# Clearing the scatter rows ahead of the FFN weights, and low parts, routing and stores reordered in a two-layer cross-attention, FFN and mixture-of-experts kernel

## Chip, cores and metric

One core of one Trainium2 chip runs the whole program in one launch. The metric is the device time in microseconds of that core. Engines: TensorE (PE), VectorE (DVE), ScalarE (ACT), GpSimd (POOL) and SyncE (SP, which only issues transfers and waits). Sixteen DMA engines serve the queues of SP, ScalarE and GpSimd.

## What is computed

Two layers over x of 2 x 256 tokens by 512, with a context of 2 x 512 by 512:

```python
x = x + xattn0(layernorm(x), ctx)   # quantised matmul
x = x + ffn0(layernorm(x))          # 4-bit block-quantised weights, 1376 wide, activations requantised
x = x + xattn1(layernorm(x), ctx)   # 32 heads, 8 KV heads, head 128, rms-normed q and k, softmax
x = x + moe1(layernorm(x))          # below

def moe1(x):                                   # 512 tokens
    scores = softmax(x @ router_w + router_b) + router_bias        # 16 experts in 4 groups
    # keep the 2 best groups, take the 2 best experts of them: idx, vals
    for e in range(16):                        # inner width 128
        h = silu(x @ w1[e] + b1[e]) * (x @ w2[e] + b2[e])
        y += gate[:, e, None] * (h @ w3[e] + b3[e])
    z = silu(x @ sw1 + sb1) * (x @ sw2 + sb2) @ sw3 + sb3          # shared expert, inner width 256
    return y + z
```

The FFN's weights are in reference form `w_gate`, `w_up` (1376, 512) and `w_down` (512, 1376).

## The kernel before

All float32 products are split: an operand is a 16-bit high part and a 16-bit low part, and `product` makes three matmuls (high x high, high x low, low x high). A high part is a copy by ScalarE, a low part is the difference, by VectorE or GpSimd. Every engine runs its own program in order, and semaphores join them. SBUF is one tensor, `arena`, cut by hand with `carve(kib, ...)`; tiles whose lives don't overlap share bytes.

**Start and FFN (0 to about 300 us).** SP's queue (from L379): inputs, the first of four 1 MB chunks of the k and v weights (`kw_load`), then the first `RAW` = 7 raw FFN weight tiles (`ring(n)`, 256 KB each), then `kw_load(1)`, which waits until the low part of the chunk before is made, `ring(7)`, `kw_load(2)`. Then the loop over `NCH` = 33 weight tiles (11 up, 11 gate, 11 down): `turn_w(n)` transposes the finished high and low part of tile n by DMA from `wt` (three slots, `DQ`) into `wfx`, `ring(n + 8)` loads a raw tile, and for n < 23 a *clear* follows: `sp.dma_start(blocks[n], blank)` writes 256 KB of zeros, DRAM to DRAM, into 128 rows of `xs_d`, the buffer into which tokens are scattered later (`blank` is a 32-row padding block of zeros in the weights, broadcast four times; `blocks[n]` is seen as 4 x 32 x 512). On the compute engines a tile goes: block maxima (VectorE), divide (GpSimd), round (ScalarE twice), `scale_back` (GpSimd), `weight_high` (ScalarE), low (VectorE, or GpSimd), `turn_w`, then TensorE's `tile`: 4 products, 12 matmuls of 128 x 512. `v_unit`s and `k_unit`s (12 matmuls each too) stand between tiles; seven of the v units stand between the first and the last of the 22 up and gate tiles. `parameters(k)` (spread on TensorE, L1199 and L1201) needs the extrema of all tiles of a matrix.

**Attention (about 300 to 657 us).** 32 steps (8 KV heads x 4 token tiles) in a loop; each has scores, softmax over VectorE, ScalarE and GpSimd, high and low parts of the probabilities (`p_high`, `p_low`), four DMA transposes (`turn_p`) and the products. Between steps (7, 1) and (7, 2) VectorE prepares the router weights and the experts' biases (L1917 to L1928).

**Experts and routing (about 640 to 700 us).** `EX` = 18 expert weight sets of 768 KB (two shared, sixteen routed) come into `ER` = 4 raw slots `me_raw` (`load_experts(n)` waits for the low part of n - 4), and get a high part (`expert_high`, ScalarE) and a low part: of those in `POOL_LOW` = (0, 1, 4, 7, 13, 15, 17) by GpSimd (which scales first), of the others by VectorE (`expert_lows`). After the last attention step VectorE makes the statistics, `expert_norm` writes `xn`, which shares bytes with the probabilities and so waits for their last transposes; TensorE transposes it, `router`, `logits`, `scores`, `choose` (the two best experts and their one-hot rows `chosen`), `earlier` (how many tokens stand before one with the same expert), `place` (the row of each token, `places`). TensorE works on the shared experts' `shared_hidden` between them. GpSimd scatters each token's row to two places (`spread_rows`, 8 indirect transfers) once all clears are in (`filled`).

**Blocks (about 700 to 781 us).** 23 blocks of 128 rows: `x_load(i)` transposes a block from `xs_d` (four slots; the first waits for the whole scatter), TensorE `tile_hidden(i)`, ScalarE `tile_sigmoid`, VectorE `tile_gate`, ScalarE `tile_hidden_high`, VectorE `tile_low`, TensorE `tile_out`, ScalarE `tile_result` into one of three `yb`, SP `y_store`. Beside blocks 0 to 9 the remaining experts' parts are made: ScalarE takes expert i + 9 after block i. Then GpSimd gathers two result rows a token, VectorE adds them, and SP stores `out`.

Of the kernel before, what the change touches and what calls it, by code (L numbers as in the profile page):

```python
# [15 lines left out]
P = 128  # L16
# [40 lines left out]
ER = 4  # L57
SC = 8
POOL_LOW = (0, 1, 4, 7, 13, 15, 17)
# [76 lines left out]
def block_kernel(nc, x, ctx, ctx_t, quant_par, ident_in, ffn_w, kv_w, mask, norm_w, wq, wo,  # L136
                 router_w, router_b, moe_w, moe_b, moe_b3, tri_in, out):
    es = ExitStack()
    with es:
# [81 lines left out]
        gt = carve(202, (1, TOK))  # L221
# [7 lines left out]
        xs = [carve(k, (2, D), F16) for k in (36, 38, 190, 192)]  # L229
        xg = [carve(194 + 2 * i, (2 * KD, P), F16) for i in range(XB)]  # L230
# [8 lines left out]
        pick_f, iota_1 = carve(102, (NE,)), carve(102.25, (NE,))  # L239
# [139 lines left out]
        def _(sp):  # L379
# [33 lines left out]
            kw_load(0)  # L413
            for n in range(RAW):
                ring(n)
            kw_load(1)
            ring(RAW)
            kw_load(2)

# [101 lines left out]
            def y_store(i):  # L521
                sp.wait_ge(t_ev, i + 1)
                sp.dma_start(y_d[i * P:(i + 1) * P], yb[i % YB]).then_inc(y_st[i % YB], 16)

# [12 lines left out]
            for i in range(TILES - XB - 3, TILES):  # L537
                y_store(i)
# [7 lines left out]
        def _(g):  # L546
# [200 lines left out]
            def expert_scale(n):  # L747
                g.wait_ge(in_me[n % ER], 16 * (n // ER + 1))
                g.tensor_scalar(me_raw[:, n % ER], me_raw[:, n % ER], SW, 1.0, ALU.mult, ALU.mult).then_inc(m_sc, 1)

            def expert_low(n):
                g.wait_ge(m_hi, high_count(n))
                g.tensor_tensor(me[n][:, 1], me_raw[:, n % ER], me[n][:, 0], ALU.subtract).then_inc(m_lo[0], 1)

# [28 lines left out]
            def xs_low(t):  # L783
                g.wait_ge(xs_hi, t + 1)
                g.tensor_tensor(xs[t][:, 1], xn[:, t], xs[t][:, 0], ALU.subtract).then_inc(xs_lo, 1)
# [8 lines left out]

            expert_scale(4)
            expert_low(4)
            rstd(6, 0, NT - 1)
            expert_scale(7)
            for t in range(NT - 1):
                xs_low(t)  # L800
            rstd(7, NT - 1, NT)
            expert_low(7)
# [5 lines left out]
            for n in (13, 15, 17):  # L808
                expert_scale(n)
                expert_low(n)  # L810
# [9 lines left out]
        def _(a):  # L820
# [265 lines left out]
            expert_high(4)  # L1086
            expert_high(5)

            def xs_high(t):
                a.wait_ge(h_nm, NT + t + 1)  # L1090
                copy(xs[t][:, 0], xn[:, t]).then_inc(xs_hi, 1)
# [11 lines left out]
            expert_high(6)  # L1103
# [7 lines left out]
            expert_high(7)  # L1111
# [38 lines left out]

            for i in range(TILES):
# [4 lines left out]
                if i + 9 < EX:  # L1156
                    expert_high(i + 9)
            for i in range(TILES - 3, TILES):
                tile_result(i)


        @block.tensor
        def _(pe):
# [239 lines left out]
            def expert_transposes(t):  # L1403
                pe.wait_ge(h_nm, NT + t + 1)
                for k in range(KD):
                    mm = pe.transpose(bank(t)[:, k * P:(k + 1) * P], xn[:, t, k * P:(k + 1) * P], ident[:, :])
# [47 lines left out]
            expert_transposes(NT - 1)  # L1454
            pe.wait_ge(h_lo, 2 * NT)
            router(NT - 1, NT)
            for i in range(2):
                shared_hidden(0, i, TOK - P, TOK)
            pe.wait_ge(m_lo[0], 2)
            shared_hidden(1, 0, 0, TOK)  # L1460
            pe.wait_ge(const_v, 4)
            pe.wait_ge(r_oh, 1)
            for t in range(NT - 1):
                earlier(t)
            pe.wait_ge(r_oh, 2)
# [4 lines left out]
            shared_hidden(1, 1, 0, TOK)  # L1470
# [63 lines left out]
        def _(v):  # L1534
# [336 lines left out]
            def attention_step(j, s):  # L1871
# [8 lines left out]
                for h in range(R):  # L1880
                    v.wait_ge(a_e, 4 * u + h + 1)
# [9 lines left out]
                final = isinstance(j, int) and u == HK * NT - 1  # L1891
                for h in range(R):
                    if final and h == 2:
                        o_low(u - 1)
                    p_low(u, h)
                if not final and (not isinstance(j, int) or u >= 1):
# [10 lines left out]
            for s in range(5):  # L1907
                attention_step(0, s)
# [5 lines left out]
            attention_step(HK - 1, 1)  # L1914

            v.wait_ge(in_mp, 16 * 5)
            own.mark(v.memset(flat(bias_raw), 0.0))  # L1917
            own.link(v.tensor_reduce(iota, tri, AX.X, ALU.add))
            own.mark(ts(later_row, iota, -float(P), ALU.mult, float((NE - 1) * P), ALU.add))
            own.link(ts(flat(mbs[:, :, :]), flat(mb[:, :, :]), SXW, ALU.mult))  # L1920
            own.link(v.tensor_copy(bias_raw[:, :, 0:NE], mb[:, :, NS:EX]))
            v.tensor_copy(bias_raw[:, :, 32:32 + NE], mb[:, :, NS:EX]).then_inc(r_ws, 1)
            own.mark(ts(b3[0:NE + 1, 0], b3[0:NE + 1, 0], SXW, ALU.mult))
            own.link(ts(flat(rw_raw), flat(rw_raw), SW, ALU.mult))
            v.tensor_copy(flat(rw[0]), flat(rw_raw)).then_inc(r_ws, 1)
            v.wait_ge(r_ws, 2)
            tt(flat(rw[1]), flat(rw_raw), flat(rw[0]), ALU.subtract).then_inc(r_ws, 1)

            attention_step(HK - 1, 2)
# [18 lines left out]
            def expert_norm(k, lo, hi):  # L1948
                v.wait_ge(rstd_ready, k + 1)
                for t in range(lo, hi):  # L1950
                    ts(xn[:, t], xres[:, t], mv[:, t, 0:1], ALU.subtract, rs[:, t:t + 1], ALU.mult).then_inc(h_nm, 1)
# [24 lines left out]
            def choose(lo, hi):  # L1976
                n = hi - lo
# [5 lines left out]
                own.wait(own.n)  # L1983
                own.link(v.tensor_copy(at[:, lo:hi], best_at[:, lo:hi, 0:2]))
# [30 lines left out]
            own.mark(ts(pick, pick_f, SW, ALU.mult))  # L2015
            for t in range(3):
# [5 lines left out]
            expert_norm(7, 3, 4)  # L2022
# [4 lines left out]
            own.link(ts(iota_1, iota, 1.0, ALU.add))  # L2027
            own.link(tt(pick_f, pick_f, iota_1, ALU.mult))
            own.link(v.tensor_reduce(part, pick_f, AX.X, ALU.add))
# [152 lines left out]
```

## Time and profile before

| | |
|---|---|
| runs, median (lowest to highest) | 811.12 us (808.1 to 814.69) |
| the profiled execution | 807.26 us, span 805.4 us |
| busy: TensorE, VectorE, GpSimd, ScalarE | 647.5 (80%), 626.9 (78%), 531.1 (66%), 494.0 us (61%) |
| share of 16 DMA engines, SP's queue | 63.3% of the span |

The page gives the span in 40 slices of about 20 us, one digit of busy tenths each; TensorE's are at 9 from slice 17 to slice 31. "PEclk" is TensorE's granted clock. A wait "[4.01 <-DVE ...]" is the engine's idle time before an instruction and what ended it. Transfers on a queue have no duration as such: the SP timeline shows the time in which SP issued them, and "us to landing" is from the issue to the semaphore.

### The profile page before, as it was taken

To read this page: it belongs to the slowest core of one execution; us is meant where nothing else is said; L and a number is where in the kernel's file an instruction comes from. 1 tells how busy PE (TensorE), PEld (TensorE's weight loads), DVE (VectorE), ACT (ScalarE), POOL (GpSimd) and SP (SyncE) were. 2 spreads that over 40 slices of the span, in tenths; PEclk is the share of its full clock that TensorE was granted. 3 is DMA by queue.
4 is the path that set the end of the run, shared out by engine and by line. 5 is a ranking of instruction groups with operands and counts; after the bars stand their busy time and mean duration, and the time that the engine had idled before them with its cause. 6 is when DMAs were issued, how large, how long until landed. Compare 5 with 4: busy or idle time off the path is not lost.

```text
span 805.4 us, 12660 instructions
## 1 busy us (share of the span) xinstructions
PE 647.5 (80%) x3432; PEld 316.6 (39%) x3432; DVE 626.9 (78%) x1331; ACT 494.0 (61%) x986; POOL 531.1 (66%) x505
## 2 busy tenths in 40 slices
PE   0595898846395996999999999999999868676870
PEld 0242343312132442444444444444444335254650
DVE  6896687788899678788888888888888876476622
ACT  4564665659757437777777777777777763145430
POOL 1897586887666557788788888888888744405004
PEclk9899999988688898999999999999999988888995
DMA  8326999992434315877766667666645670499944
GB/s 342 103 81 83 188 188 202 178 166 53 92 59 93 123 58 146 179 169 180 181 142 143 149 156 156 156 143 143 143 92 104 109 244 1 138 289 271 218 145 157
DMA packets 231272, 120.12 MB, mean 149 GB/s; under 512 B 213933, under 2 KB 214189, under 8 KB 228286
## 3 DMA queue, kind: packets, MB, share of 16 engines
q1 hardware_dynamic: 229950, 115.42, 63.3%
q0 software_dynamic: 1280, 4.20, 1.6%
q8 instruction: 20, 0.33, 0.2%
q14 instruction: 22, 0.18, 0.1%
HBM read 57.97 MB, written 15.20 MB: 91 GB/s over the span
## 4 chain that ended last, share of the span: by engine, by line
PE 49%; DVE 20%; DMA 9%; issue 8%; POOL 7%; ACT 4%; SPq 2%; POOLq 0%; DVEq 0%; ACTq 0%
PE ps L1166 16%; PE ps L1168 15%; PE ps L1167 15%; DVE arena L1541 5%; DVE arena L1544 4%; DMA arena<-arena 3%; ACT arena L822 3%; DVE arena L1538 2%; DMA y_d<-arena 2%; POOL arena L594 1%; PE ps L1334 1%; DMA arena<-in_moe_w 1%; POOL arena L586 1%; DVE ss L1691 1%; DMA arena<-in_ffn_w 1%
## 5 line engine op out<-in xcount | busy, mean ns | idle before, releaser
L1166 PE MATMUL ps<-arena 128*128 128x512 f16 (+2 forms) x1011 | 360.6, 361 | 74.2 <-DMA arena<-arena 26.0
L1167 PE MATMUL ps<-arena 128*128 128x512 f16 (+2 forms) x1011 | 359.6, 360 | 0.0
L1168 PE MATMUL ps<-arena 128*128 128x512 f16 (+2 forms) x1011 | 358.6, 359 | 0.0
L822 ACT ACTIVATE arena<-arena 128x512 f16<-128x512 f32 (+8 forms) x404 | 249.2, 649 | 88.1 <-POOL arena L767 29.6
L1166 PEld LDWEIGHTS ps<-arena 128*128 128x128 f16 (+1 forms) x1011 | 102.1, 101 | 191.8 <-issue 51.0
L1538 DVE TENSOR_TENSOR arena<-arena 128x512 f16<-128x512 f32 (+3 forms) x163 | 126.6, 807 | 22.5 <-ACT arena L822 22.2
L1168 PEld LDWEIGHTS ps<-arena 128*128 128x128 f16 (+1 forms) x1011 | 102.5, 101 | 102.2 <-issue 9.8
L1167 PEld LDWEIGHTS ps<-arena 128*128 128x128 f16 (+1 forms) x1011 | 102.3, 101 | 90.4 <-issue 7.2
L767 POOL TENSOR_SCALAR arena<-arena,rden 128x512 f32<-128x512 f32 x128 | 114.5, 894 | 16.1 <-DVE rden L1884 6.8
L1044 ACT ACTIVATE arena<-arena,mneg 128x512 f32<-128x512 f32 x124 | 88.6, 715 | 35.1 <-DVE mneg L1864 35.1
L822 ACT ACTIVATE arena<-ps 128x512 f16<-128x512 f32 (+2 forms) x105 | 58.7, 587 | 52.6 <-PE ps L1168 29.5
L1864 DVE CUSTOM_DVE_ANT_0 arena<-ps,arena 128x512 f32<-128x512 f32 x128 | 82.9, 685 | 3.4 <-issue 0.3
L715 POOL TENSOR_TENSOR arena<-arena 128x512 f32 (+1 forms) x64 | 73.3, 1165 | 8.1 <-ACT arena L822 8.1
L1544 DVE SCALAR_TENSOR_TENSOR arena<-arena 128x128 f16<-128x128 f32 (+7 forms) x62 | 54.0, 887 | 26.7 <-DMA arena<-y_d,places 15.6
L730 POOL TENSOR_TENSOR rk<-ss,nh 128x4 f32<-128x4 f32 x32 | 32.6, 1018 | 50.1 <-DVE ss L1541 50.0
L710 POOL TENSOR_SCALAR arena<-arena 128x512 f32<-128x512 f32 x64 | 60.3, 955 | 2.4
L1544 DVE SCALAR_TENSOR_TENSOR arena<-ps,arena 128x512 f16<-128x512 f32 (+3 forms) x80 | 52.0, 655 | 7.0 <-ACT arena L822 4.7
L594 POOL TENSOR_TENSOR arena<-arena,dsc 128x512 f32<-128x512 f32 x33 | 38.8, 1176 | 6.6 <-ACT arena L822 6.6
L1538 DVE TENSOR_TENSOR arena<-ps,arena 128x128 f32<-128x128 f32 (+2 forms) x51 | 16.1, 319 | 34.4 <-ACT arena L1137 32.7
L586 POOL TENSOR_TENSOR arena<-arena,dsi 128x512 f32<-128x512 f32 x33 | 37.0, 1121 | 5.8 <-DVE dsi L1582 5.8
L815 POOL DMA_INDIRECT arena<-y_d,places x8 | 8.6, 1072 | 41.8 <-DMA y_d<-arena 39.7
L1541 DVE TENSOR_SCALAR arena<-arena,aqp 128x512 int32<-128x512 f32 x48 | 34.4, 721 | 0.3
(156 smaller groups left out, 722.5 us busy)
## 6 DMA issues: line engine op xcount, KB each, us to landing
arena<-in_moe_w SPq DMA_DIRECT2D x18, 768.0 KB, 5.5
arena<-in_ffn_w SPq DMA_DIRECT2D x33, 256.0 KB, 6.0
arena<-in_wq SPq DMA_DIRECT2D x8, 1024.0 KB, 5.1
arena<-in_wo SPq DMA_DIRECT2D x8, 1024.0 KB, 5.1
xs_d<-in_ffn_w SPq DMA_DIRECT2D x23, 256.0 KB
y_d<-arena SPq DMA_DIRECT2D x23, 256.0 KB, 3.0
arena<-in_kv_w SPq DMA_DIRECT2D x4, 1024.0 KB, 7.6
arena<-arena SPq DMA_TRANSPOSE x177, 3.3
```

The source lines that it names most:

```text
L710: g.tensor_scalar(src, src, SW, 1.0, ALU.mult, ALU.mult).then_inc(aw_sc, 1)
L715: g.tensor_tensor(lo, src, hi, ALU.subtract).then_inc(aw_lo, 1)
L767: g.tensor_scalar(sc[:, h], sc[:, h], rden[:, h:h + 1], SP, ALU.mult, ALU.mult)\
L822: return a.activation(out_, in_, ACT.Copy, scale=scale, bias=bias)
L1044: a.activation(sc[:, h], sc[:, h], ACT.Exp, bias=mneg[:, h:h + 1], scale=-1.0, accum_out=den[:, h:h + 1]).then_inc(a_e, 1)
L1166: pe.matmul(out_, lhs[0], rhs[0], start=first, stop=False)
L1167: pe.matmul(out_, lhs[0], rhs[1], start=False, stop=False)
L1168: return pe.matmul(out_, lhs[1], rhs[0], start=False, stop=last)
L1538: return v.tensor_tensor(out_, x_, y_, op)
L1541: return v.tensor_scalar(out_, x_, s1, s2, o1, o2)
L1544: return v.scalar_tensor_tensor(out_, x_, s_, y_, o1, o2)
L1864: v.tensor_tensor_reduce(sc[:, h], bank(h), mk[:, t % 2], -1.0 / SXW, 3.0e38, ALU.add, ALU.min, mneg[:, h:h + 1]).then_inc(a_sm, 1)
```

## The change

- **Clears**: out of the weight loop; 7 behind the seventh raw load, 8 behind `kw_load(1)`, 8 behind `kw_load(2)`, all ahead of `turn_w(0)`.
- **Low parts**: `POOL_LOW` is (0, 1) only; experts 2 to 7 are done by VectorE behind the routing and the shared hidden parts, 8 to 17 one per block. High parts on ScalarE follow.
- **Five raw slots**: `ER` = 5. `load_experts(5)` stands ahead of the last `turn_p`, then 4 (whose slot shares bytes with attention operands) and 6 to 12, all ahead of SP's wait for the scatter.
- **Routing**: the norm writes `xe_n` (108 KB, free by then) in three pieces of 2, 1 and 1 tiles; the one-hot rows (`mark`) are split from `choose`; TensorE leaves the last token tile's columns of all shared products for after the counts; small operands are made elsewhere.
- **Bias and router operands**: spread over attention steps (0, 1) to (0, 4), (7, 1) and (7, 2), each ahead of the last reciprocal of the step.
- **Last attention step**: the four `p_high` and `p_low` are no longer interrupted by an expert's high part or `o_high`, `o_low`.
- **Stores**: `y_store(i)` is issued from ScalarE's queue, behind block i + 3's work.

```diff
-ER = 4
+ER = 5
-POOL_LOW = (0, 1, 4, 7, 13, 15, 17)
+POOL_LOW = (0, 1)
...
             for n in range(RAW):
                 ring(n)
+            clear(0, 7)
             kw_load(1)
+            clear(7, 15)
             ring(RAW)
             kw_load(2)
+            clear(15, TILES)
...
-                if n < TILES:
-                    sp.dma_start(blocks[n], blank).then_inc(filled, 16)
...
             turn_p(HK - 1, 2)
+            load_experts(5)
+            turn_p(HK - 1, 3)
+            sp.wait_ge(a_y, HK * NT - NT)
             load_experts(4)
-            turn_p(HK - 1, 3)
-            for n in range(5, 9):
+            for n in range(6, 13):
                 load_experts(n)
...
-            for n in range(9, 12):
-                load_experts(n)
             for i in range(TILES - XB):
                 x_load(i + XB)
-                if i + 12 < EX:
-                    load_experts(i + 12)
-                if i >= 3:
-                    y_store(i - 3)
+                if i + 13 < EX:
+                    load_experts(i + 13)
...
              for h in range(R):
-                if h == 2:
-                    expert_high(2)
-                    o_high(last - 1)
                 p_high(last, h)
+            o_high(last - 1)
+            expert_high(2)
             expert_high(3)
...
             shared_sigmoid(0)
-            expert_high(8)
+            shared_sigmoid(1)
+            expert_high(5)
+            expert_high(6)
             shared_high(0)
-            shared_sigmoid(1)
+            expert_high(7)
             a.wait_ge(g_t, 1)
             copy(gt[0:NE + 1, 0], bank(0)[0:NE + 1, :]).then_inc(g_c, 1)
             shared_high(1)
+            for n in range(8, 12):
+                expert_high(n)
...
                 tile_hidden_high(i)
-                if i + 9 < EX:
-                    expert_high(i + 9)
+                if i + 12 < EX:
+                    expert_high(i + 12)
+                if i >= 3:
+                    y_store(i - 3)
...
+            pe.wait_ge(m_lo[0], 2)
+            shared_hidden(1, 0, 0, TOK - P)
             pe.wait_ge(h_lo, 2 * NT)
             router(NT - 1, NT)
-            for i in range(2):
-                shared_hidden(0, i, TOK - P, TOK)
-            pe.wait_ge(m_lo[0], 2)
-            shared_hidden(1, 0, 0, TOK)
...
             earlier(NT - 1).then_inc(r_rank, 1)
-            shared_hidden(1, 1, 0, TOK)
+            for n in range(NS):
+                for i in range(2):
+                    shared_hidden(n, i, TOK - P, TOK)
...
-            expert_lows(2)
             stats(0, 2)
-            expert_lows(3)
+            variance(0, 2)
             add_out(HK - 1, 2)
             stats(2, 3)
-            variance(0, 3)
-            for h in range(R):
-                v.wait_ge(turned[h], 16 * HK * NT)
-            expert_norm(6, 0, 3)
-            o_low(HK * NT - 1)
+            variance(2, 3)
+            expert_norm(6, 0, 2)
+            expert_norm(7, 2, 3)
...
+            v.wait_ge(xs_lo, NT)
             shared_hidden(0)
             gates()
+            expert_lows(2)
             shared_low(0)
             shared_hidden(1)
+            expert_lows(3)
             shared_low(1)
-            expert_lows(5)
-            expert_lows(6)
+            for n in range(4, 8):
+                expert_lows(n)
...
-                if i in beside:
-                    expert_lows(beside[i])
                 tile_low(i)
+                if i + 8 < EX:
+                    expert_lows(i + 8)
```

## Rows read from the trace of the kernel before

**Rows 1.** Windows view: us, busy time (instructions) per engine, PEclk, DMA share, GB/s

```profile
30.00:35.00 5.00, 1.27 (x6) 0.39 (x4) 4.00 (x8) 2.56 (x4) 5.00 (x5) 0.96 0.00 0
150.00:160.00 10.00, 7.32 (x35) 2.96 (x32) 8.12 (x13) 6.83 (x12) 10.00 (x10) 1.00 0.94 166
```

**Rows 2.** SP's timeline, 0 to 160 us: start, us, queue, line, operation, count

```profile
4.03 21.33 SPq L395 DMA_DIRECT2D arena<-in_ffn_w  x7
36.89 0.33 SPq L404 DMA_DIRECT2D arena<-in_kv_w  x1
...
56.02 0.33 SPq L404 DMA_DIRECT2D arena<-in_kv_w  x1
67.99 1.35 SPq L410 DMA_TRANSPOSE arena<-arena  x1
...
70.00 0.85 SPq L431 DMA_DIRECT2D xs_d<-in_ffn_w  x1
```

**Rows 3.** DMA view, 70 to 100 us, in 40 slices of 0.75 us

```profile
DMA  9689231349992295992269924299922699222992
GB/s 170 180 187 119 79 71 66 99 104 332 281 153 98 99 235 99 296 200 109 98 156 318 327 106 108 93 300 309 195 106 101 153 321 313 109 98 93 293 273 98
```

**Rows 4.** Windows view, half a microsecond inside one clear

```profile
99.50:100.00 0.50, 0.50 (x4) 0.20 (x2) 0.50 (x2) 0.50 (x2) 0.38 (x1) 1.00 0.25 98
```

**Rows 5.** Source view of the weight transposes (L410): 135 to 171, 171 to 215 us

```profile
DMA to landing us min/median/max: 3.9/5.6/7.1
...
DMA to landing us min/median/max: 3.0/3.1/5.0
```

**Rows 6.** TensorE's timeline: tile 0, tile 4, the next unit, the gate's spread

```profile
71.29 0.38 PE L1166 MATMUL ps<-arena 128*128 128x512 f16 x1 [1.57 <-DMA arena<-arena]
...
90.86 0.39 PE L1166 MATMUL ps<-arena 128*128 128x512 f16 x1 [1.35 <-DMA arena<-arena]
93.46 0.38 PE L1166 MATMUL ps<-arena 128*128 128x512 f16 x1
...
176.92 0.37 PE L1199 MATMUL ps<-ident,ext 128*2 128x128 f32 x1 [5.09 <-DVE ext L1654]
```

**Rows 7.** Waits, 71 to 171 us: us in total, times, longest

```profile
PE ps L1166 <- DMA arena<-arena: 20.5, 15, 3.9
```

**Rows 8.** VectorE's timeline, 626 to 686 us

```profile
627.74 0.27 DVE L1917 MEMSET arena<- 128x256 f32 x1
...
629.71 0.23 DVE L1538 TENSOR_TENSOR arena<-arena 128x64 f16<-128x64 f32 x1
...
652.93 3.86 DVE L1544 SCALAR_TENSOR_TENSOR arena<-arena 128x1536 f16<-128x1536 f32 x1
...
670.02 3.31 DVE L1541 TENSOR_SCALAR arena<-arena,mv,rs 128x512 f32<-128x512 f32 x1 [0.32 <-POOL rs L556]
...
682.22 0.17 DVE L1541 TENSOR_SCALAR arena<-ps 128x16 int32<-128x16 f32 x1 [3.09 <-PE ps L1467]
...
684.72 0.17 DVE L1544 SCALAR_TENSOR_TENSOR places<-arena 128x8 int32<-128x8 f32 x1
```

**Rows 9.** The chain that ended last, 700 to 760 us: start, us, what

```profile
715.66 1.68 DVE arena L1544
...
726.79 3.99 DVE arena L1544
```

**Rows 10.** Page (loads to landing); timelines of SP and ScalarE, 699 to 780 us

```profile
arena<-in_moe_w SPq DMA_DIRECT2D x18, 768.0 KB, 5.5
...
699.62 5.55 SPq L519 DMA_TRANSPOSE arena<-xs_d  x4
...
705.75 0.28 ACT L1137 ACTIVATE arena<-ps 128x128 f32<-128x128 f32 x1 [15.35 <-PE ps L1504]
...
710.83 1.48 ACT L822 ACTIVATE arena<-arena 128x1536 f16<-128x1536 f32 x1 [3.81 <-DMA arena<-in_moe_w]
...
779.39 0.28 ACT L1137 ACTIVATE arena<-ps 128x128 f32<-128x128 f32 x1 [1.23 <-PE ps L1504]
```

More of the change, by code:

```diff
@@ L228, in block_kernel @@
         gsc = carve(165.953125, (NT, 2))
-        xs = [carve(k, (2, D), F16) for k in (36, 38, 190, 192)]
-        xg = [carve(194 + 2 * i, (2 * KD, P), F16) for i in range(XB)]
+        xs = [carve(k, (2, D), F16) for k in (36, 38, 150, 152)]
+        xg = [carve(196 + 2 * i, (2 * KD, P), F16) for i in range(XB)]
+        xe_n = carve(108, (NT, D))
         yb = [carve(k, (D,)) for k in (100, 102, 162)]
@@ L413, in _, with clear @@
             kw_load(0)
+            def clear(lo, hi):
+                for n in range(lo, hi):
+                    sp.dma_start(blocks[n], blank).then_inc(filled, 16)
             for n in range(RAW):
                 ring(n)
+            clear(0, 7)
             kw_load(1)
+            clear(7, 15)
             ring(RAW)
             kw_load(2)
+            clear(15, TILES)
             def turn_k(u):
@@ L1405, in expert_transposes @@
                 for k in range(KD):
-                    mm = pe.transpose(bank(t)[:, k * P:(k + 1) * P], xn[:, t, k * P:(k + 1) * P], ident[:, :])
+                    mm = pe.transpose(bank(t)[:, k * P:(k + 1) * P], xe_n[:, t, k * P:(k + 1) * P], ident[:, :])
                 mm.then_inc(h_ps, 1)
@@ L1869, in p_low, with attention_step @@
                 tt(ph[:, h, 1], sc[:, h], ph[:, h, 0], ALU.subtract).then_inc(a_pl, 1)
-            def attention_step(j, s):
+            def attention_step(j, s, beside=None):
                 u, t = 4 * j + s, s % 4
@@ L1880, in attention_step @@
                 for h in range(R):
+                    if beside and h == R - 1:
+                        beside()
                     v.wait_ge(a_e, 4 * u + h + 1)
@@ L1890, in attention_step @@
                     tile_low(NT - 1)
-                final = isinstance(j, int) and u == HK * NT - 1
                 for h in range(R):
-                    if final and h == 2:
-                        o_low(u - 1)
                     p_low(u, h)
-                if not final and (not isinstance(j, int) or u >= 1):
+                if not isinstance(j, int) or u >= 1:
                     o_low(u - 1)
@@ L1906, in _, with bias_rows, bias_columns, out_biases @@
             tile_norm(3)
-            for s in range(5):
-                attention_step(0, s)
+            def bias_rows():
+                v.wait_ge(in_mp, 16 * 5)
+                own.mark(v.memset(flat(bias_raw), 0.0))
+                ts(flat(mbs[:, :, :]), flat(mb[:, :, :]), SXW, ALU.mult)
+            def bias_columns():
+                own.mark(v.tensor_copy(bias_raw[:, :, 0:NE], mb[:, :, NS:EX]))
+                v.tensor_copy(bias_raw[:, :, 32:32 + NE], mb[:, :, NS:EX]).then_inc(r_ws, 1)
+            def out_biases():
+                own.mark(ts(b3[0:NE + 1, 0], b3[0:NE + 1, 0], SXW, ALU.mult))
+            def router_scaled():
+                own.mark(ts(flat(rw_raw), flat(rw_raw), SW, ALU.mult))
+                own.mark(v.tensor_reduce(iota, tri, AX.X, ALU.add))
+            def router_high():
+                v.tensor_copy(flat(rw[0]), flat(rw_raw)).then_inc(r_ws, 1)
+                own.mark(ts(later_row, iota, -float(P), ALU.mult, float((NE - 1) * P), ALU.add))
+            def router_low():
+                v.wait_ge(r_ws, 2)
+                tt(flat(rw[1]), flat(rw_raw), flat(rw[0]), ALU.subtract).then_inc(r_ws, 1)
+            attention_step(0, 0)
+            attention_step(0, 1, bias_rows)
+            attention_step(0, 2, bias_columns)
+            attention_step(0, 3, out_biases)
+            attention_step(0, 4, router_scaled)
             def four_steps(j):
@@ L1913, in _ @@
             own.loop(1, HK - 1, 4, four_steps)
[L1914 to L1929, printed above, removed]
+            attention_step(HK - 1, 1, router_high)
+            attention_step(HK - 1, 2, router_low)
             attention_step(HK - 1, 3)
@@ L2026, in _ @@
             logits(3, 4, 1)
-            own.link(ts(iota_1, iota, 1.0, ALU.add))
-            own.link(tt(pick_f, pick_f, iota_1, ALU.mult))
-            own.link(v.tensor_reduce(part, pick_f, AX.X, ALU.add))
-            own.link(ts(part, part, -1.0, ALU.add))
+            mark(0, 3)
             scores(3, 4, 1)
             choose(3, 4)
+            mark(3, 4)
+            own.mark(v.memset(gts[:, :, 0:NS], 1.0))
+            own.mark(ts(gsc, best[:, :, 0:2], 1.0 / SXW, ALU.mult))
             place()
@@ L2050, in gates @@
                 tops = best[:, :, 0:2]
-                own.mark(v.memset(gts[:, :, 0:NS], 1.0))
-                own.mark(ts(gsc, tops, 1.0 / SXW, ALU.mult))
                 own.link(tt(where, chosen, tops.unsqueeze(3).broadcast_to([P, NT, 2, NE]), ALU.mult))
                 tt(gts[:, :, NS:EX], where[:, :, 0], where[:, :, 1], ALU.add).then_inc(gates_ready, 1)
+            v.wait_ge(xs_lo, NT)
             shared_hidden(0)
             gates()
+            expert_lows(2)
             shared_low(0)
             shared_hidden(1)
+            expert_lows(3)
             shared_low(1)
-            expert_lows(5)
-            expert_lows(6)
+            own.link(ts(iota_1, iota, 1.0, ALU.add))
+            own.link(tt(pick_f, pick_f, iota_1, ALU.mult))
+            own.link(v.tensor_reduce(part, pick_f, AX.X, ALU.add))
+            own.link(ts(part, part, -1.0, ALU.add))
+            for n in range(4, 8):
+                expert_lows(n)
             def extra_tiles():
```

54 lines of the change are left out of this document (19 added, 35 removed).

## The prediction

> **What bounds the kernel now.** I read the page first: TensorE is busy 80% of the span, and its digits of the forty slices stand at 9 from about 320 to 625 us alone. In that attention stretch it has no room to give, and the change takes nothing from it. The edits lie in the loads at the start, the FFN stretch, the last attention step, the routing, and the 23 expert blocks.
>
> *Start.* The windows view shows the DMA engines doing nothing at 30 to 35 us [rows 1], and the SP queue's timeline shows why: after the seven first raw loads (issue ends at 25.4 us) SP waits for results, and sends only one wk/wv chunk at 36.9, another at 56.0 and, at 68.0, the first weight transpose [rows 2]. That is the room into which the change puts 23 clears.
>
> *FFN.* From 70 to 100 us the DMA view alternates between full bars and bars of 2 tenths at about 98 GB/s, one such dip per FFN tile [rows 3]; a half-microsecond window inside one dip has share 0.25 and 98 GB/s [rows 4]. Those dips are the clears: a quarter of the 16 engines works, which is what the source's outermost dimension of 4 (the zero block repeated four times) gives. So a clear of 262 KB takes 262/98 = 2.67 us, and what stands behind it on SP's queue waits: a weight transpose lands in 5.6 us while clears run between them, in 3.1 us once they are over [rows 5]. TensorE starts its first tile at 71.29 and another at 90.86, four later: 4.9 us each, where the twelve matmuls of a tile need 93.46 - 90.86 = 2.60 us [rows 6]. Over 71 to 171 us its matmuls waited 20.5 us for these transposes [rows 7]. The stretch ends at VectorE's extrema, at 176.92.
>
> *Tail.* VectorE's timeline and the chain show two costs around the routing: the low parts of experts 2 and 3 stand ahead of the norm, and an instruction of VectorE takes 3.86 or 3.31 us where GpSimd multiplies or subtracts beside it [rows 8]; a 1536-wide low part takes 1.68 us alone and 3.99 beside GpSimd [rows 9].
>
> **The change, part by part.**
>
> *Clears moved ahead.* Seven go behind the seventh raw load, eight behind the chunk of 36.9 us, eight behind that of 56.0. Nothing is removed: 23 x 2.67 = 61.4 us of a quarter of the engines, and every load and transpose here uses all 16, so each waits at the clears before it. In order on those four engines, with the first clear's data 2 us after its issue (an estimate from the 3.1 us in which an undisturbed transpose is issued, run and reported): 7 clears from 27.4 to 46.1; the chunk, 1,049 KB at four times the dip's rate (4 x 98 = 392 GB/s), 2.7 us, to 48.8; 8 clears to 70.2; raw load 7 and the third chunk, 0.7 + 2.7, to 73.6; the last 8 clears, 21.4, to 95.0. Only then comes the first weight transpose, issued at 68 as before: with 2.0 us more to run and report (3.1 from issue to landing when undisturbed [rows 5], 1 of them before the data), TensorE's first tile starts at 97.0 instead of 71.3, **+25.7**. That the second chunk comes 7 us late delays GpSimd's scaling and the v units behind it, but all of it is over well before 95.0 and hides there. Bounds: nothing, if successive clears run beside each other on other engines (a rival below); +30 if some clears run slower.
>
> What is given back: with no clears between tiles, the queue holds about 0.7 (raw load) + 1.3 (transpose, my estimate from the same 3.1) per tile, under TensorE's 2.6. The most that can come back is TensorE's idle time. From tile 0 to the end of the gate tiles it has 22 tiles and 7 v units, 29 x 2.60 = 75.4 us of work; in before this took from 71.29 to 176.92 - 5.09 = 171.8, so 25.1 us were idle [rows 6], 20.5 of them on transposes [rows 7]. I take 15.0 back, not 20.5: GpSimd is busy for 10.00 of 10.00 us at 150 to 160 [rows 1], so the later transposes are also late because their weights are, and after 20 us without work the ring of three weight slots has to fill again. Ends: 8 (only the first ten tiles gain) and 23.8 (TensorE almost without a gap). **Net of the stretch: 25.7 - 15.0 = +10.7**, between +1.9 and +18. What comes after (gate, product, down projection) is a chain of results and starts later by as much.
>
> By the Trainium skill, "DMA: Bandwidth & Descriptors", section "Rules for kernel authors", a transfer whose outermost dimension is a repeat of c copies stays on at most c engines, and the section "Why a DMA increments its semaphore by 16 and not by 1" adds that from SP's queue these are always the lowest-numbered ones. The first half is what the bars show; the second no row here can show, as no two clears of before run back to back. With the second the sum stays +10.7; without it the clears would need 23 x 0.67 = 15.4 us, and the first rival below would hold.
>
> *Bias and router operands.* Ten small VectorE instructions between attention steps (from 627.74 to 629.94, 2.2 us [rows 8]) go into steps 0 to 4 and two late steps. There they stand where VectorE waits for an exponential anyway. TensorE did not stop at once for them; I take **-1.2** at the end, and +0.7 in the first steps, where nobody is at 100% yet. Ends: 0 and -2.2; 0 and +2.2.
>
> *Last step and routing.* The norm no longer waits behind the two low parts (1.68 + 3.86), its own copy no longer takes 3.31 instead of about 0.7 (GpSimd's low part beside it is gone), and TensorE's counts no longer stand behind shared-expert products, for which VectorE waited 3.09 [rows 8, 9]. Together 1.7 + 3.9 + 2.6 + 3.1 = 11.3: the places, ready at 684.9 now [rows 8], come 11 us sooner relative to the attention, and the scattered rows with them.
>
> *What is late next.* SP must issue the loads of experts 6 to 12 before it waits for the scatter, and load n waits for the low part of expert n - 5. The low parts of 2 to 7 now all stand on VectorE behind the places, and the order has a link through the loads: low 2, then load 7 (5.5 us to land [rows 10]), then ScalarE's high part 7 (1.48 [rows 10]), then the second shared hidden, and only then lows 4 to 7. From places at 673.9 (in before's times): shared hidden, gates and low 2 to 678.4; load 7 to 684.4; high 7 and two copies to 687.1; shared low and four small ones to 688.6; four lows at 1.68 to 695.3. Load 12 is issued then and x transpose 0 after it, at 696 where it was 699.62 [rows 10], and it runs behind 10 to 12, three loads of 786 KB. So block 0's sigmoid comes at 705, where it came at 705.75 [rows 10]: **-0.7** of the 11 arrives. Ends: -8 if the loads are quick, +3.
>
> *Blocks.* GpSimd's five low parts go, VectorE's no longer take 3.99; the store issues from ScalarE cost it perhaps 0.6 us a block, under waits. But ScalarE's high part 13 at block 1 waits for load 13, which waits for low 8 behind block 0: 1.68 + 5.5 + 1.48 = 8.7, and some 1.5 of sigmoid, gate and copies, 10 us per two blocks until block 5, then 2.7 a block by VectorE, then TensorE. I come to 74 us from sigmoid 0 to 22; before has 779.39 - 705.75 = 73.6 [rows 10]. **0**, between -6 and +6. The final gather and sums stay.
>
> **Sum.** +10.7 - 1.2 + 0.7 - 0.7 + 0 = **+9.5 us** on the profiled execution's own 807.26 (span 805.4): 816.8. The median of the runs shown is 811.12, 3.9 above that execution; on it the forecast is 820.6.
>
> **The rivals.**
>
> *Clears do not queue.* If the clears use different engines in turn, or run beside the loads, all 23 are over by 68 us; the FFN starts on time and gives the 15 to 20 us: 811.1 - 15 - 0.5 - 0.7 - 0 = about 795. For it: the queue is empty for most of 25 to 68 us. Against it: every dip in [rows 3] has the depth of four engines, and transposes land later beside them [rows 5]. It decides if the first transpose lands before about 82 us.
>
> *The routing's gain gets through.* If low 4 to 7 and the loads do not hold SP, block 0 starts 8 us sooner; with the FFN loss the result is 820.6 - 7.3 = 813, no measurable change.
>
> *The block stage becomes load-bound too.* High parts waiting for loads at 10 us per two blocks or more, up to block 7: +6 more, 827.
>
> *Nothing is moved, only renamed.* The FFN stretch loses at its start exactly what it gains later (savings near 23.8): +1.9 there, 812.
>
> **How the numbers follow.** A few measured rounds of this kernel separate about 1%, 8.1 us: below 803.0 is faster, above 819.2 slower. The forecast's own mechanism (late first tile, part given back, routing's gain lost) has 0.50, with its own range of 813 to 831; clears that do not queue 0.15; the routing's gain through 0.15; renamed 0.08; a load-bound stage 0.12. Slower takes most of the first (0.43) and the fifth, 0.55; within 1% the rest of the first, the third and the fourth, 0.30; faster 0.15. The range 803 to 834 leaves out the first rival below and some 0.05 above.
>
> **What would show it.** Late first tile: TensorE's first line-L1166 tile after the v units near 97, the DMA share near 0.25 from about 27 to 46 and from 74 to 95 us, the first transpose 25 us or more from issue to landing. Given back: transposes landing in about 3.1 us from then on, tiles 2.6 to 3.9 us apart, the 20.5 us of [rows 7] below 6. Routing: places ready 11 us sooner after the last attention step, SP's first transpose from xs_d right after load 12. Stage: ScalarE's waits on in_moe_w over 10 us. The forecast is wrong if the clears show up at 90% of the engines, each under 1 us, or if SP has issued the first xs_d transpose within 2 us of the last scatter.

## The result and the profile after

The changed kernel takes 820.45 us (median of 4 runs, 819.89 to 820.86), the kernel before 809.61 beside it on the same chip (806.67 to 814.69): ratio 1.0152, 95% interval 1.0108 to 1.0196. It is slower, by 1.5%. The span of the profiled execution grew from 805.4 to 818.6 us, **+13.2**.

SP's timeline of the changed kernel, 0 to 110 us (start, us, queue, line, operation, count), answers to [rows 2]; L417 are the clears, L411 the weight transposes:

```profile
26.27 10.54 SPq L417 DMA_DIRECT2D xs_d<-in_ffn_w  x7
38.06 1.21 SPq L405 DMA_DIRECT2D arena<-in_kv_w  x1
39.31 20.73 SPq L417 DMA_DIRECT2D xs_d<-in_ffn_w  x8
60.17 2.33 SPq L396 DMA_DIRECT2D arena<-in_ffn_w  x1
...
63.13 20.47 SPq L417 DMA_DIRECT2D xs_d<-in_ffn_w  x8
83.64 5.95 SPq L411 DMA_TRANSPOSE arena<-arena  x1
...
91.71 3.09 SPq L411 DMA_TRANSPOSE arena<-arena  x1
```

Its DMA view, 20 to 100 us in slices of 2 us, answers to [rows 3]:

```profile
DMA  3584122223972222222225972222222292222897
GB/s 65 212 261 128 53 100 102 102 101 107 271 311 102 109 110 101 102 102 102 102 102 164 346 287 102 107 103 102 102 101 102 102 154 101 102 102 100 221 323 195
```

TensorE's timeline (first FFN tile after the v units, spread of the gate) answers to [rows 6]; then the windows view (us, busy time per engine, PEclk, DMA share, GB/s) and the waits over 71 to 200 us, which answer to [rows 7]:

```profile
96.02 0.59 PE L1157 MATMUL ps<-arena 128*128 128x512 f16 x1 [25.91 <-DMA arena<-arena]
...
189.80 0.37 PE L1190 MATMUL ps<-ident,ext 128*2 128x128 f32 x1 [5.95 <-DVE ext L1646]
```

```profile
74.00:95.00 21.00, 0.00 (x0) 0.00 (x0) 3.28 (x6) 1.26 (x2) 6.74 (x7) 0.50 0.72 109
...
80.00:84.00 4.00, 0.00 (x0) 0.00 (x0) 0.00 (x0) 0.00 (x0) 1.07 (x2) 0.50 0.26 102
...
85.00:86.00 1.00, 0.00 (x0) 0.00 (x0) 0.00 (x0) 0.00 (x0) 0.00 (x0) 0.50 9.50 207
...
98.00:100.00 2.00, 2.00 (x6) 0.76 (x5) 0.00 (x0) 0.00 (x0) 0.00 (x0) 0.50 0.71 195
...
102.00:104.00 2.00, 2.00 (x11) 0.88 (x9) 1.43 (x3) 1.69 (x4) 0.20 (x1) 1.00 0.00 0
```

```profile
PE ps L1157 <- DMA arena<-arena: 31.2, 5, 25.9
```

The reader sees three plateaus of 100 to 110 GB/s, one for each batch of clears: the last runs to 94 us. Behind it stands the first weight transpose, and TensorE starts 24.7 us later than before (96.02 against 71.29). At the gate's spread 12.9 of these are left.

The tail, in the changed kernel's timelines of VectorE, SP and ScalarE, 655 to 795 us; they answer to [rows 8] and [rows 10]:

```profile
685.62 0.17 DVE L1536 SCALAR_TENSOR_TENSOR places<-arena 128x8 int32<-128x8 f32 x1
...
697.78 0.69 DVE L1536 SCALAR_TENSOR_TENSOR arena<-arena 128x512 f16<-128x512 f32 x1 [4.13 <-ACT arena L806]
```

```profile
661.22 45.16 SPq L484 DMA_DIRECT2D arena<-in_moe_w  x8
706.42 11.91 SPq L527 DMA_TRANSPOSE arena<-xs_d  x5
```

```profile
695.27 1.48 ACT L806 ACTIVATE arena<-arena 128x1536 f16<-128x1536 f32 x1 [5.96 <-DMA arena<-in_moe_w]
...
717.10 0.28 ACT L1121 ACTIVATE arena<-ps 128x128 f32<-128x128 f32 x1 [4.53 <-PE ps L1496]
...
746.30 1.48 ACT L806 ACTIVATE arena<-arena 128x1536 f16<-128x1536 f32 x1 [5.11 <-DMA arena<-in_moe_w]
...
792.28 0.28 ACT L1121 ACTIVATE arena<-ps 128x128 f32<-128x128 f32 x1 [1.39 <-PE ps L1496]
```

The places are ready 0.9 us later than before (685.62 against 684.72), though everything ahead of them was 10.8 us late; yet block 0's sigmoid is 11.35 us late (717.10 against 705.75). What the routing gained was lost again within the 31.5 us between these two rows, which were 21.0 before.

### The profile page after: what moved, and what is told of

The parts are those of the page before. It is cut to its first block, busy times and chain, and to the rows that moved or that the text cites. A ratio compares the mean times of both kernels' runs of the same rounds, so it can differ in the third digit from the quotient of the medians.

```text
span 818.6 us, 12704 instructions
## 1 busy us (share of the span) xinstructions
PE 650.6 (79%) x3455; PEld 320.1 (39%) x3456; DVE 623.7 (76%) x1337; ACT 496.1 (61%) x986; POOL 509.8 (62%) x496
## 4 chain that ended last, share of the span: by engine, by line
PE 52%; DVE 14%; DMA 11%; POOL 10%; issue 6%; ACT 4%; SPq 3%; POOLq 0%; ACTq 0%; DVEq 0%
PE ps L1157 17%; PE ps L1159 16%; PE ps L1158 16%; DVE arena L1536 4%; ACT arena L806 3%; DMA arena<-arena 3%; DMA arena<-in_moe_w 3%; SPq L417 2%; DVE arena L1530 2%; DVE arena L1533 2%; POOL arena L571 2%; POOL arena L592 2%; DMA arena<-in_ctx_t 2%; DMA arena<-in_kv_w 2%; PE ps L1325 1%
## 5 line engine op out<-in xcount | busy, mean ns | idle before, releaser
L1157 PE MATMUL ps<-arena 128*128 128x512 f16 (+3 forms) x1019 | 363.5, 361 | 91.2 <-DMA arena<-arena 35.2
L1158 PE MATMUL ps<-arena 128*128 128x512 f16 (+3 forms) x1019 | 363.0, 361 | 0.0
L1159 PE MATMUL ps<-arena 128*128 128x512 f16 (+3 forms) x1019 | 362.0, 360 | 0.0
L1157 PEld LDWEIGHTS ps<-arena 128*128 128x128 f16 (+1 forms) x1019 | 103.6, 102 | 205.3 <-issue 77.4
L1159 PEld LDWEIGHTS ps<-arena 128*128 128x128 f16 (+1 forms) x1019 | 103.8, 102 | 102.9 <-issue 12.1
L1158 PEld LDWEIGHTS ps<-arena 128*128 128x128 f16 (+1 forms) x1019 | 103.6, 102 | 93.7 <-issue 11.0
L1536 DVE SCALAR_TENSOR_TENSOR arena<-arena 128x1536 f16<-128x1536 f32 (+5 forms) x67 | 50.9, 780 | 31.0 <-DMA arena<-y_d,places 15.9
L1566 DVE TENSOR_REDUCE dsc<-arena 128x16 f32<-128x512 f32 x33 | 21.4, 659 | 19.3 <-DMA arena<-in_ffn_w 19.2
```

The lines of the kernel that those rows point to most:

```text
L1157: pe.matmul(out_, lhs[0], rhs[0], start=first, stop=False)
L1158: pe.matmul(out_, lhs[0], rhs[1], start=False, stop=False)
L1159: return pe.matmul(out_, lhs[1], rhs[0], start=False, stop=last)
L1536: return v.scalar_tensor_tensor(out_, x_, s_, y_, o1, o2)
```

## The experiments

Every ratio is to the kernel before, timed beside it; where two changed kernels are compared by their times, they were not all timed together. A time within one profile also varies without an edit: five kernels below have the same start and FFN with wide clears, and their gate's spread stands between 162.71 and 165.88 us. In the diffs the names are those of the changed kernel.

**1. The clears alone, each way.** Is the loss all from the clears, or do the other parts carry some? One kernel puts the clears of the changed kernel back into the weight loop, one for each tile behind its raw load:

```diff
-            clear(0, 7)
...
-            clear(7, 15)
...
-            clear(15, TILES)
...
+                if n < TILES:
+                    sp.dma_start(blocks[n], blank).then_inc(filled, 16)
```

> Everything of the change but the clears, which stand behind the weight transposes again, one per tile. If the loss is the queue of clears ahead of the first transpose (theory Q), the first tile of TensorE is back at about 71 us, the extrema of the gate at about 177, and the time is that of before within 3 us, about 809: the profiles of before and after differ by 13.0 us at that point and by 13.2 at the end. If the loss lay in the expert stage (theory L: loads and high parts), it stays, 818 to 821.

Measured: 806.33 us, ratio 0.9993 (0.9967 to 1.0019); the gate's spread is back at 175.64 us (176.92 before). The other takes the kernel before and moves its clears ahead, nothing else:

> The kernel before with nothing changed but the place of the 23 clears. Theory Q: first tile at about 96 us, gate's extrema 13 us late, and the time 809.6 + 13 = 822 to 823, somewhat above the changed kernel. Theory L: no measurable change, 807 to 812.

Measured: 820.28 us, ratio 1.0165 (1.0114 to 1.0216), its first tile at 95.85 us behind a wait of 25.75. I had expected 822 to 823. So the clears' new place is the whole loss, and all the rest of the change together, in the order in which it stands, is worth nothing that can be measured. Experiment 4 shows that parts of it cancel.

**2. The clears walked wide.** If the price comes of four engines' worth of rate, the same bytes walked with 32 as the outermost count should cost almost nothing, ahead or in the loop:

```diff
-            blank = ffn_w[F % P:, FT - 1].unsqueeze(0).broadcast_to([P // F_PAD, F_PAD, D])
-            blocks = [... .rearrange("(a b) d -> a b d", b=F_PAD) for i in range(TILES)]
+            blank = ffn_w[F % P:, FT - 1].unsqueeze(1).broadcast_to([F_PAD, P // F_PAD, D])
+            blocks = [... .rearrange("(a b) d -> b a d", b=F_PAD) for i in range(TILES)]
```

> The changed kernel, but each clear walks 32 x 4 x 512 in place of 4 x 32 x 512 (same bytes, same places in the queue, outermost dimension 32), so all 16 engines can share it. If the four engines are the cause (Q), a clear takes about 0.7 us in place of 2.67, 23 take 15.4 us, all in the idle room, the first tile is at 70 to 73 us, transposes land in about 3.1 us, and besides the 13 us of the FFN some 10 more come back: 820.5 - 13 - 12 = about 796, range 791 to 802. If it is the number of bytes or of rows written to HBM that costs, and not the engines that carry them, it stays at 817 to 821.

Measured, on the changed kernel: 794.29 us, ratio 0.9855 (0.9808 to 0.9903).

> The kernel before, clears in their old place, walked 32 x 4 x 512. Q: per tile the queue holds 0.7 + 0.7 + 1.3 us in place of 4.7, the transposes land in about 4 us, TensorE's 20.5 us of waits for them fall below 8, and the time is 809.6 - 11 = about 799, range 795 to 803. If bytes or rows cost: 807 to 812.

Measured, on the kernel before: 794.40 us, ratio 0.9857 (0.9813 to 0.9900), just under the range of 795 to 803 that I had given. From 71 to 165 us TensorE's matmuls waited 8.0 us for the transposes, which landed in 3.6 us (median). SP's timeline and the DMA view of the first of the two, 20 to 100 us:

```profile
56.79 5.10 SPq L417 DMA_DIRECT2D xs_d<-in_ffn_w  x8
68.39 1.36 SPq L411 DMA_TRANSPOSE arena<-arena  x1
```

```profile
DMA  4567898007999600045799901991839979770099
GB/s 117 172 238 189 281 272 303 3 0 156 402 395 381 251 0 0 0 102 94 332 390 404 363 24 30 172 283 45 140 119 176 161 197 156 201 168 0 20 185 204
```

The plateaus are gone, eight clears are issued in 5.10 us instead of 20.47, and the first transpose leaves SP at 68.39, as before. The gate's spread stands at 165.02 us (164.73 with the wide clears in the loop), against 176.92 before and 189.80 after. These two kernels differ in the rest of the change too, but all of that stands behind the gate's spread, and there they are 0.3 us apart. Once the clears are wide, their place makes no difference that shows; the gain comes from how they are walked.

**3. Half wide.** Does the time follow the sum of the clears' durations, or something else? The same clears as 8 by 16 rows:

```diff
+            blank = ffn_w[F % P:F % P + 16, FT - 1].unsqueeze(0).broadcast_to([P // 16, 16, D])
+            blocks = [... .rearrange("(a b) d -> a b d", b=16) for i in range(TILES)]
```

> The changed kernel (820.4 us) with the same clears ahead, walked as 8 by 16 rows instead of 4 by 32 (wide, 32 by 4, gave 794.3). Theory (a clear goes to as many engines as its outermost dimension, at about 25.5 GB/s each, and the start pays for the queued time): a clear takes 1.34 us instead of 2.67, steady 204 GB/s while they run, 30.7 us in all instead of 61.4. The slope between the two known kernels (26 us of time for 45 us of queued clears) gives 802 to 804 us. Rival (the cost comes of many descriptors or of the transposes behind them, not of idle engines): 815 to 820.

Measured: 795.75 us, ratio 0.9854 (0.9808 to 0.9900). Its DMA view, 20 to 100 us:

```profile
DMA  2684355555955555224965555799554897782058
GB/s 57 228 252 127 111 195 194 194 204 114 393 207 195 192 204 204 105 51 129 348 259 199 197 193 203 211 215 237 100 160 95 198 134 198 175 161 101 0 113 200
```

The rate is as the theory had it, twice the narrow one (195 to 204 GB/s against 102), but the slope of 0.58 us for each queued microsecond was wrong: I expected 802 to 804. What counts is only the backlog that is left when the first transpose is issued. With 1.3 us a clear (an estimate, 262 KB at 204 GB/s) the three batches fit into the room between the raw loads and 70 us, the transpose leaves SP at 69.92, and the gate's spread comes at 166.12, only 1.1 us behind that of the wide clears, hardly beyond what the same stretch varies by. A price that falls to nothing at a threshold can't be read off a line between two points.

**4. Where the routing's lead goes.** In the runs so far the change's tail and the tail of before came out equal at each kind of clears (820.45 and 820.28 narrow, 794.29 and 794.40 wide), though the places came 13.6 us sooner with the narrow clears (685.62 against 699.21) and 9.6 sooner with the wide ones (662.40 against 671.98). Two links were suspected. First the one by way of the loads: low 2, load 7, high 7, shared low, lows 4 to 7, load 12.

```diff
             shared_high(0)
-            expert_high(7)
             a.wait_ge(g_t, 1)
...
             shared_high(1)
-            for n in range(8, 12):
+            for n in range(7, 12):
                 expert_high(n)
```

> The changed kernel with wide clears (794.3 us), and ScalarE's high part of expert 7 moved from ahead of shared_high(1) to behind it. Theory (the routing's lead is eaten where VectorE's lows stand behind shared_low(1), which waits 4.13 us for ScalarE): that wait falls to about 1 us or less, lows 4 to 7 end, load 12 and x_load 0 come about 3 us sooner (680 instead of 683.2), block 0's sigmoid at about 691 instead of 694, the time about 791. Rival (another thing sets block 0, the routing's own descriptors or the loads' landings): x_load 0 moves, but the time stays 794 within 1 us.

Measured: 792.50 us, ratio 0.9811 (0.9788 to 0.9834). VectorE's wait of 4.13 us is gone, and load 12 is issued 5.3 us sooner (677.85, end of the row below, against 683.16). But x_load 0 did not move (683.42 against 683.20), where theory and rival both had it move. Block 0's sigmoid came 2.9 us sooner all the same (691.10 against 694.02), 7.7 us behind x_load 0 instead of 10.8, which fits the loads ahead of it having been issued 5 us earlier. The time of 792.50 lies between the theory's 791 and the rival's 794, and whether it is under 794.29 at all isn't clear, as the two intervals overlap. Rows of SP and GpSimd:

```profile
637.24 40.61 SPq L484 DMA_DIRECT2D arena<-in_moe_w  x8
683.42 8.90 SPq L527 DMA_TRANSPOSE arena<-xs_d  x5
```

```profile
675.31 1.36 POOL L781 DMA_INDIRECT xs_d<-arena,places  x1 [0.30 <-issue]
```

Now it waits for the scatter: 6.75 us from GpSimd's last row to the transpose. So there is a second obstacle behind the first. The next kernel takes both away; the high parts of experts 9 to 11 have to move with their loads:

```diff
-            for n in range(6, 13):
+            for n in range(6, 9):
                 load_experts(n)
...
+            for n in range(9, 13):
+                load_experts(n)
...
-            for n in range(7, 12):
+            for n in range(7, 9):
                 expert_high(n)
...
-                if i + 12 < EX:
-                    expert_high(i + 12)
+                if i + 9 < EX:
+                    expert_high(i + 9)
```

> As the kernel before it in this call, and SyncE issues x_load 0 to 3 ahead of loads 9 to 12 again, as in the kernel before, with the high parts of experts 9 on taken one per block. Theory (x_load 0 stands behind load 12 on SyncE): x_load 0 directly after the scatter of the places, about 13 us behind the places, 8 us sooner than 683.2; block 0's sigmoid about 8 us sooner than 694. If the block stage is set by TensorE, the time is about 786; if the later weight loads set the early blocks (rival), the lead is given back in blocks 0 to 5, by ScalarE waits on in_moe_w over 5 us, and the time is 790 to 795.

Measured: 782.08 us, ratio 0.9691 (0.9646 to 0.9735): the fastest of all. Its rows of VectorE, GpSimd, SP and ScalarE:

```profile
660.39 0.17 DVE L1537 SCALAR_TENSOR_TENSOR places<-arena 128x8 int32<-128x8 f32 x1
```

```profile
674.48 1.36 POOL L783 DMA_INDIRECT xs_d<-arena,places  x1 [0.31 <-issue]
```

```profile
636.22 32.55 SPq L484 DMA_DIRECT2D arena<-in_moe_w  x4
677.61 5.54 SPq L527 DMA_TRANSPOSE arena<-xs_d  x4
683.19 2.45 SPq L484 DMA_DIRECT2D arena<-in_moe_w  x4
```

```profile
683.81 0.28 ACT L1122 ACTIVATE arena<-ps 128x128 f32<-128x128 f32 x1 [8.74 <-PE ps L1497]
```

The DMA views of the kernel with high 7 moved and of this one, 660 to 690 us in slices of 0.75 us:

```profile
DMA  0000035046899996989999999999999969349997
```

```profile
DMA  0000440687989989999851700695969699999999
```

In the first the bars stand at 9 from 673.5 to 684 us: loads 9 to 12 were issued from 672.51 to 677.52, and their 3.15 MB take 7.7 us at the 410 GB/s that the view shows there (an estimate). In the second they fall to 1, 7, 0, 0 at 675.75 to 678.75, around x_load 0. Here it follows GpSimd's last scatter by 1.8 us instead of 6.75, and the places by 17.2 us instead of 22.2 (14.9 in the kernel before). From x_load 0 to block 0's sigmoid it is 6.2 us (6.1 before [rows 10], 10.7 after, 10.8 with wide clears alone). The block stage, sigmoid 0 to 22, takes 70.1 us (683.81 to 753.87) where it took 72.6 with the wide clears alone, so nothing of the lead was given back. I had expected 786, by a sigmoid 8 us sooner; it came 10.2 sooner, and the stage added 2.5. ScalarE's longest wait for a weight load in the stage was 4.10 us, under the 5 that the rival needed.

This kernel is the rest of the change with SP's old order of x loads and weight loads, and with high 7 moved. It stands about 12 us under the kernel before with wide clears (ratios 0.9691 and 0.9857, intervals apart). So the rest of the change is worth that much where the order is kept, and nothing where it isn't. How its parts share it was not measured.

**5. Is the move of high part 7 needed too?** The same kernel with `expert_high(7)` ahead of `shared_high(1)` again.

> The kernel of 782.1 us (x loads ahead of loads 9 to 12, wide clears) with the high part of expert 7 back ahead of shared_high(1). Theory (with x_load 0 no longer behind load 12 the lows 4 to 7 don't matter to block 0): x_load 0 still 17 us behind the places, 782 within 1.5 us, though VectorE waits 4 us before shared_low(1) again. Rival (the lows set blocks 0 to 5 too): 785 or more.

Measured: 783.58 us, ratio 0.9696 (0.9643 to 0.9749). The places stand 17.2 us ahead of x_load 0 in both, though GpSimd's last scatter ends 3.2 us ahead of it here and 1.8 there; sigmoid 0 follows by 7.8 us instead of 6.2. VectorE's wait is back, 4.21 us. The order of the x loads, with the high parts that go with it, carries the gain; whether the other part adds 1.5 us, these runs can't tell.

**6. Do the two causes add?** The order of experiment 4 on the changed kernel's narrow clears.

> The changed kernel with its narrow clears ahead (820.4 us) and only the tail changed: x loads ahead of loads 9 to 12, high 7 behind shared_high(1), the high parts one per block from 9 on. Theory (two separate causes that add): 820.4 less the 12.2 us that the same edit gave on wide clears, 808 within 2.5 us; block 0's sigmoid about 8 to 10 us sooner than 717.1. Rival (the gain needs the wide clears): 815 or more.

Measured: 807.46 us, ratio 0.9992 (0.9967 to 1.0018), 13.0 us under the changed kernel, where the same edit gave 12.2 on wide clears. They add. But the way there differs from what I expected: block 0's sigmoid came at 712.03, only 5.1 us sooner, and the block stage took 67.8 us instead of 75.2. Part of that is no effect of the edit: ahead of the tail, in which all of it stands, this profile was already late (the places at 687.25 against 685.62), where the one with wide clears was early (660.39 against 662.40). Counted from the places the sigmoid came 6.7 us sooner here and 8.2 there. Why the stage gave 7.4 here and 2.5 on wide clears isn't settled by these runs.

**7. The stores.** The kernel with wide clears, and `y_store` issued from SP as before.

```diff
+                if i >= 3:
+                    y_store(i - 3)
...
-                if i >= 3:
-                    y_store(i - 3)
```

> The changed kernel with wide clears (794.3 us), and the results' stores on SyncE's queue again. Theory (the move of the stores is worth nothing in sum): 794 within 1.5 us, block stage 72.6 us from sigmoid 0 to sigmoid 22 within 1.5. Rival (a store on SyncE holds up the x loads behind it): the block stage longer by 3 us or more, 797 and over.

Measured: 792.67 us, ratio 0.9823 (0.9792 to 0.9854), against 0.9855 (0.9808 to 0.9903) with the stores on ScalarE's queue. Block stage 71.75 us against 72.6. The move is worth nothing that shows.

All of it in one table, ratios to the kernel before:

| clears | tail of before | tail of the change | with x loads first |
| --- | --- | --- | --- |
| narrow, in the loop | 1 | 0.9993 | |
| narrow, ahead | 1.0165 | 1.0152 | 0.9992 |
| 8 by 16, ahead | | 0.9854 | |
| wide, ahead | 0.9857 (in the loop) | 0.9855 | 0.9691 |

## Why the prediction was right, step by step

The forecast was 820.6 us, the time 820.45. The two steps that carry it, the clears' queue and the routing's lost lead, held as mechanisms. The larger terms were off by 1 to 3 us each, and the fit of the total is better than that of its parts (last point).

- **A clear takes 2.67 us on a quarter of the engines, and clears queue.** Held. The plateaus stand at 102 GB/s, 262 KB / 102 = 2.57 us each, and never run beside each other. Of the marks I had named, the bars stand at 2 tenths and the windows' share is 0.26 at 80 to 84 us. Over 74 to 95 us it is 0.72, but that comes from one microsecond, 85 to 86, where the view gives a share of 9.50, though 1 would be all sixteen engines; so it is no reading of how many work, and the GB/s beside it (109) is the number to go by. By the Trainium skill, "DMA: Bandwidth & Descriptors", section "Why a DMA increments its semaphore by 16 and not by 1", the number of engines is the largest count up to 16 that divides the outermost dimensions of both sides. The runs agree at 4 (102 GB/s) and 8 (204 GB/s), and at 32, where the rule gives 16, the slice of 42 to 44 us, behind the weight chunk, shows 395 GB/s. The first rival, that clears spread over different engines (795 us), is refuted by the plateaus alone.
- **First tile at 97.0, +25.7.** Measured 96.02, +24.7. One thing on the way was not in the working: I let SP issue the transpose at 68 and wait in the queue for 29 us. In fact SP's own issue was held up, 20.47 us for eight clears against 5.10 wide, and the transpose left SP at 83.64 and landed 12.2 us later, not the 25 or more that I had named as a mark. The sum of both is the same, since the engines' backlog is what lasts.
- **15.0 us given back.** Measured 11.8 (24.7 less the 12.9 at the gate's spread). TensorE's waits for transposes did fall, from 20.5 us [rows 7] to 5.3 beside the first, and the transposes landed in 3.1 us (median, 106 to 185 us) as described. The term was a choice between 8 and 23.8, and 3.2 too large. Two things stand in rows that it had no place for: the wait at the gate's spread grew by 0.9 (5.95 against 5.09), and after 25.9 us without work TensorE's granted clock was 0.50 (1.2 GHz) until about 101.2 us, so the first 13 matmuls took 5.43 us, where 13 at the later 0.216 us each take 2.81: 2.6 us more.
- **Bias and router operands, -1.2 and +0.7.** From the gate's spread to SP's expert load ahead of the attention's last four transposes it is 465.9 us before, 463.9 after: -2.0. With the clears back in the loop it was -0.2, with wide clears -1.0 against its counterpart. The term of -0.5 lies among them; its size stays open, as these differences are no larger than what one profile varies by.
- **Places 11 us sooner.** Measured 9.9 (10.8 late at that same load, 0.9 late at the places).
- **-0.7 of the 11 arrives at block 0.** Held: relative to that load the sigmoid came +0.5. SP's x_load 0 stood right behind load 12 (706.38 and 706.42), and VectorE's 4.13 us behind ScalarE's high 7, which waited 5.96 for load 7, was the link described. I had x_load 0 at 696 and block 0 at 705 in before's times, so 9 us between them, behind three loads; measured 10.7, behind four (9 to 12, issued from 701.04 to 706.05). What I did not see is that removing this link would not have been enough: with it gone (experiment 4) the scatter's own landing took 6.75 us instead of 1.8, where the DMA view stood at 9 tenths throughout. With loads 9 to 12 issued behind the x loads that wait was 1.8, 3.2 and 2.5 us in three kernels (experiments 4, 5 and 6). That they delay it is shown by this; that they do so by filling the DMA engines is read from the two views in experiment 4.
- **Block stage, 0.** Measured 75.2 us against 73.6, +1.5. ScalarE's waits on in_moe_w were 5.11 us at most, not over 10, so the stage was bound by loads less than described. The rival of a load-bound stage (827) has little for it: five such waits, 13.8 us together.
- **Sum.** +12.9 - 2.0 + 0.5 + 1.5 = +12.9 of the span's +13.2, where the forecast had +9.5, so on profiled executions it was 3.7 us short, 2.2 of them in the FFN stretch. By medians the kernels stand 10.8 us apart (809.61 and 820.45), and it was 1.3 short. That it hit the time itself to 0.2 us is owed to the median on which it was laid, 811.12, which is 1.5 above the one measured beside the changed kernel.

The likeliest case was right; the rival that the routing's gain gets through (813) would have taken the other order of SP's queue, and that version, still with its narrow clears, measured 807.46.

## What to carry to other kernels

Look at what a transfer does to its queue before choosing its place: a fill that uses 4 of 16 engines cost 26 us more ahead of the first weights, and 13 more in the loop, than the same bytes walked wide, which came out the same in both places (0.9855 and 0.9857, the first with the rest of the change). A queued transfer costs the backlog that remains when the next one that someone waits for is issued, so by the three widths measured here it is a threshold, not a slope. When results come 10 us sooner and the end does not move, follow the first consumer's transfer back through its queue; here weight loads for later experts stood ahead of it, and one obstacle hid another.

## What the runs showed of the hardware

- Queued narrow transfers hold back SP itself: eight clears were issued in 20.47 us on 4 engines (2.56 each, the time of a clear), 5.76 on 8 (0.72 each, less than the 1.3 that one takes, so SP was not held), 5.10 on 16. Everything behind them in SP's program, transfers of all other kinds too, is late from its issue on: the first weight transpose left SP at 83.64 us instead of 67.99.
- TensorE's granted clock was 0.50 behind a pause of 25.9 us, and stayed there for 5.2 us of back-to-back matmuls. It cost 2.6 us.
- From the issue of the first DMA transpose of scattered rows to the first sigmoid it took 6.1 us with no weight load just ahead, and 10.7 with four of 786 KB issued in the 5.4 us before it.
